# MLP in halved products: sums moved from GpSimd to VectorE, normalisation to ScalarE, third-layer operands written by the second layer

## The reference

```python
h = layernorm(x) * (1 + ca) + sa
x = x + ga * attention(h, W_attn, W_proj)     # 16 heads, causal
h = layernorm(x) * (1 + cb) + sb
a = relu(h @ W1.T + b1)                       # 512 -> 1024
a = relu(a @ W2.T + b2)                       # 1024 -> 1024
x = x + gb * (a @ W3.T + b3)                  # 1024 -> 512
```

## Time and profile before

| | us |
|---|---|
| median of 3 runs | 1684.85 (1684.47 to 1688.04) |
| the profiled execution | 1680.77 |
| its span, first to last instruction | 1679.0 |
| PE busy in it | 1479.9 (88%) |
| DVE busy | 1056.3 (63%) |
| ACT busy | 789.9 (47%) |
| POOL busy | 830.2 (49%) |

### The profile page before, as it was taken

One profiled execution on the slowest core, in us unless ns is written; L12 is line 12 of the kernel. 1 busy time (PEld: TensorE's weight loads), 2 busy tenths in 40 slices (PEclk: granted clock), 3 DMA queues, 4 the chain that ended last, 5 costly groups with the idle time before them and its releaser, 6 DMA issues. The chain is left out here.

```text
span 1679.0 us, 30398 instructions
## 1 busy us (share of the span) xinstructions
PE 1479.9 (88%) x12112; PEld 1340.3 (80%) x12112; DVE 1056.3 (63%) x1795; ACT 789.9 (47%) x1430; POOL 830.2 (49%) x661
## 2 busy tenths in 40 slices
PE   7899999999999999746999999679999999676676
PEld 6578888888888888635888888679999999676676
DVE  4477777777777776638566555754444445865665
ACT  2166667676666666713444444443333334321221
POOL 2166756666656566726444455402222225445645
PEclk9899999999999999967999999989999999888788
DMA  6434353534343434152334444423222224343342
GB/s 215 137 84 115 90 129 89 130 89 124 90 116 95 115 90 105 44 207 88 138 138 142 151 160 160 173 85 129 101 106 109 101 101 153 111 169 139 107 166 98
DMA packets 111229, 205.21 MB, mean 122 GB/s; under 512 B 12648, under 2 KB 35176, under 8 KB 111088
## 3 DMA queue, kind: packets, MB, share of 16 engines
q1 hardware_dynamic: 107456, 200.62, 38.7%
q10 hardware_dynamic: 3632, 2.64, 0.5%
HBM read 93.61 MB, written 58.75 MB: 91 GB/s over the span
## 5 line engine op out<-in xcount | busy, mean ns | idle before, releaser
L429 POOL TENSOR_TENSOR prob_lo<-prob,prob_hi 128x512 f16<-128x512 f32 x256 | 296.9, 1165 | 137.9 <-ACT prob L533 137.6
L526 ACT ACTIVATE prob_hi<-key_score 128x512 f16<-128x512 f32 x320 | 191.1, 597 | 127.6 <-PE key_score L824 125.2
L1994 PE MATMUL sum_b<-op,w 128*128 128x256 f32 x1728 | 221.8, 287 | 14.5 <-DVE op L1663 7.3
L1994 PEld LDWEIGHTS sum_b<-op,w 128*128 128x128 f32 x1728 | 215.2, 195 | 15.5 <-DVE op L1663 7.5
L735 PE MATMUL lin<-h_parts,wqkv 128*128 128x512 f32 x768 | 217.7, 407 | 1.1 <-DVE h_parts L578 1.1
L533 ACT ACTIVATE prob<-key_score 128x512 f32<-128x512 f32 x320 | 190.8, 596 | 0.0
L697 DVE TENSOR_REDUCE row_max<-score 128x1 f32<-128x512 f32 (+2 forms) x384 | 180.3, 498 | 12.4 <-PE score L811 11.5
L735 PEld LDWEIGHTS lin<-h_parts,wqkv 128*128 128x128 f32 x768 | 142.3, 194 | 30.1 <-DVE h_parts L578 3.2
L811 PE MATMUL score<-stack 96*128 96x512 f32 (+3 forms) x512 | 155.2, 364 | 0.0
L1994 PE MATMUL sum_e<-op,w 128*128 128x256 f32 x1152 | 148.2, 286 | 5.0 <-DVE w L1751 5.0
L1994 PE MATMUL sum_a<-op,w 128*128 128x256 f32 x1152 | 147.1, 286 | 5.1 <-DVE w L1751 3.1
(11 more groups left out here) (145 smaller groups left out, 3045.3 us busy)
## 6 DMA issues: line engine op xcount, KB each, us to landing
stack<-qk_parts SPq DMA_DIRECT2D x384, 128.0 KB, 2.4
blk<-y_dram SPq DMA_DIRECT2D x64, 512.0 KB, 5.7
y_dram<-u_c SPq DMA_DIRECT2D x32, 512.0 KB, 2.9
x_tiles<-x SPq DMA_DIRECT2D x32, 256.0 KB, 3.6
attn_dram<-o_rows SPq DMA_DIRECT2D x32, 256.0 KB, 2.3
attn_tiles<-attn_dram SPq DMA_DIRECT2D x8, 1024.0 KB, 5.5
res_tiles<-x SPq DMA_DIRECT2D x8, 1024.0 KB, 8.1
x_dram<-res_tiles SPq DMA_DIRECT2D x8, 1024.0 KB, 4.4
```

Of the source, the lines that this page charges most:

```text
L429: nc.gpsimd.tensor_tensor(prob_lo[:, key[1] % 2, u, :], prob[:, u, :], prob_hi[:, key[1] % 2, u, :], ALU.subtract).then_inc(lo_pool, 1)
L526: nc.scalar.activation(prob_hi[:, q % 2, u, :], bank[:], ACT.Exp, scale=SOFTMAX_SCALE, bias=P_SHIFT)
L1994: mm = nc.tensor.matmul(dst, w[:, wl, c, cols], data[:, dl, c, :], start=begin, stop=end, skip_group_check=again)
```

## The change

What it does, piece by piece:

- All operand sums, weight sums, `add_rows`, `add_bias_rows` and `add_gated` go from POOL to DVE. POOL keeps the eight inverse deviations of 128x4.
- `normalise` goes from DVE to ACT: scale is the inverse deviation, bias is minus mean times it (`minus_means`, one small DVE instruction).
- ACT's order at the end of an expand chunk: `modulate` 2 and 3 stand ahead of the relu of block C21, not behind it.
- Layer 2 writes its result as the **seven operands of layer 3** to a new `y2_dram`: blocks C11, C21, C22 as they are (`store_made`) and four sums (`late_sums`, DVE, two pairs in the next chunk). Layer 3 only loads seven operands of 512 KB (`load_late`) and splits them; it has a buffer for each, so operand s of chunk n+1 can be loaded when product s of chunk n is done.
- Gate times b3 is added to x2 in layer 2: x2 of a chunk is loaded, added to on DVE in one instruction of 128x2048, and stored again (`X2_AT`).
- `w2_lo` and `w3_lo` stand at other places, and the sums of w3 come in two steps.

```diff
+RAW_OPS = {0: 0, 3: 2, 6: 3}
+TEMP_OPS = {4: 0, 5: 1}
...
+MADE_OPS = {0: C11, 3: C21, 5: C22}
+SUM_OPS = (2, 4, 1, 6)
+X2_AT = {B + 1: (0, 1), B + 2: (2,), B + 3: (3,), B + 4: (4,), B + 5: (5,), B + 6: (6, 7)}
...
+            def load_x2_rows(k):
+
+                if k:
+                    sp.wait_ge(xs_out, 16 * k)
+                sp.wait_ge(x2_out[k % 2], 16 * (k // 2 + 1))
+                sp.dma_start(x2[:], rows_of(x2_dram, k)).then_inc(xs_in, 16)
                 if k:
                     sp.wait_ge(gb_b3_ready, k)
                 sp.dma_start(gb_row[:], gate_dram[k:k + 1, C:2 * C].to_broadcast([P, C])).then_inc(gb_in, 16)
+
+            def store_x2_rows(k):
+                sp.wait_ge(xs_ready, k + 1)
+                sp.dma_start(rows_of(x2_dram, k), x2[:]).then_inc(xs_out, 16)
...
+            def store_made(n, s):
+
+                sp.wait_ge(relu_done, relu_no(n, MADE_OPS[s], 3) + 1)
+                sp.dma_start(y_view(y2_dram, n - B, s), made[MADE_OPS[s]][:]).then_inc(y2_out[s], 16)
+
...
+            def load_late(n, s):
+
+                k = n - CONTRACT * B
+                if k:
+                    sp.wait_ge(prod_done, done_no(n - 1, s, 0) + 1)
+                elif s in (0, 5):
+                    sp.wait_ge(op_sum, sum_no(n - 1, 3) + 1)
+                    sp.wait_ge(op_ready, op_no(n - 1, {0: 0, 5: 6}[s]) + 1)
+                elif s == 6:
+                    sp.wait_ge(op_ready, op_no(n - 1, 5) + 1)
+                else:
+                    sp.wait_ge(prod_done, done_no(n - 1, 5 if s == 2 else 4, 1) + 1)
+                sp.wait_ge(y2_out[s], 16 * (k + 1))
+                sp.dma_start(late_whole[s][:, 1], y2_dram[k, s].rearrange("p (c n) -> p c n", n=HB))\
+                    .then_inc(late_in[s], 16)
 
...
             def contract(n):
                 k = n - CONTRACT * B
+                if k == 0:
+                    for i in SUM_OPS:
+                        store_sum(n - 1, i)
+                if k + 1 < B:
+                    load_late(n + 1, 0)
+                    load_late(n + 1, 1)
                 if k:
                     store_out(k - 1, 0)
-                else:
-                    store_block(n - 1, C12)
                 if k and k + 1 < B:
                     load_gate(k + 1)
                 if k + 1 < B:
-                    load_block(n + 1, 0)
-                    load_block(n + 1, 1)
+                    load_late(n + 1, 2)
+                    load_late(n + 1, 3)
                 if k and k + 1 < B:
                     load_x2(k + 1)
                 if k + 1 < B:
-                    load_block(n + 1, 2)
-                    load_block(n + 1, 3)
+                    load_late(n + 1, 4)
+                    load_late(n + 1, 5)
+                    load_late(n + 1, 6)
                 store_out(k, 1)
 
             for k in range(B):
...
+            def normalise(k):
+                act.wait_ge(minus_mean, k + 1)
+                act.wait_ge(x2_ready, NT * (k + 1))
+                if k:
+                    act.wait_ge(aux_done, AUX_NO[(ROWS, k - 1, 3)] + 1)
+                for t in range(NT):
+                    nc.scalar.activation(xn[:, t, :], xt[:, k % 2, t, :], ACT.Identity, scale=rstd[:, t:t + 1],
+                                         bias=shift[:, t:t + 1]).then_inc(x_norm, 1)
 
...
-                    w2_hi(0)
+                if k + 1 < B:
+                    normalise(k + 1)
                 relu(n, C11)
                 hi(n, 6)
                 for c in (0, 1):
                     if k + 1 < B:
                         modulate(k + 1, c)
+                relu(n, C22)
                 if last:
-                    w2_hi(1)
-                relu(n, C22)
+                    w2_hi(0)
                 hi(n + 1, 0)
-                relu(n, C21)
                 for c in (2, 3):
                     if k + 1 < B:
                         modulate(k + 1, c)
+                relu(n, C21)
+                if last:
+                    w2_hi(1)
                 hi(n + 1, 1)
 
...
+            def add_rows(k, t):
+
+                if t == 0:
+                    dve.wait_ge(x_in[k % 2], 16 * (k // 2 + 1))
+                dve.wait_ge(proj_taken, NT * k + t + 1)
+                nc.vector.tensor_tensor(xt[:, k % 2, t], xt[:, k % 2, t], gated[:, t % 2], ALU.add)\
+                    .then_inc(x2_ready, 1)
...
+            def minus_means(k):
+
                 dve.wait_ge(rstd_ready, k + 1)
                 if k:
-                    dve.wait_ge(aux_done, AUX_NO[(ROWS, k - 1, 3)] + 1)
-                for t in range(NT):
-                    nc.vector.tensor_scalar(xn[:, t, :], xt[:, k % 2, t, :], mean_var[:, t, 0:1], rstd[:, t:t + 1],
-                                            ALU.subtract, ALU.mult).then_inc(x_norm, 1)
+                    dve.wait_ge(x_norm, NT * k)
+                nc.vector.scalar_tensor_tensor(out=shift[:], in0=mean_var[:, :, 0], scalar=-1.0, in1=rstd[:],
+                                               op0=ALU.mult, op1=ALU.mult).then_inc(minus_mean, 1)
...
+            def first_op_sum(n):
+
+                block_wait(dve, n, 1)
+                block_wait(dve, n, 0)
+                if n:
+                    dve.wait_ge(op_ready, op_no(n - 1, 4) + 1)
+                nc.vector.tensor_tensor(temp_view(n, 0), block(n, 1), block(n, 0), ALU.subtract).then_inc(op_sum, 1)
...
+            def second_op_sums(n):
+                block_wait(dve, n, 3)
+                ring_wait(dve, n, 1)
+                dve.wait_ge(op_sum, sum_no(n, 0) + 1)
+                nc.vector.tensor_tensor(op_whole(n, 1), block(n, 3), temp_view(n, 0), ALU.subtract).then_inc(op_sum, 1)
+
+                block_wait(dve, n, 2)
+                if n:
+                    dve.wait_ge(op_ready, op_no(n - 1, 5) + 1)
+                dve.wait_ge(op_sum, sum_no(n, 1) + 1)
+                nc.vector.tensor_tensor(temp_view(n, 1), op_whole(n, 1), block(n, 2), ALU.subtract).then_inc(op_sum, 1)
+
+            def third_op_sum(n):
+                ring_wait(dve, n, 2)
+                nc.vector.tensor_tensor(op_whole(n, 2), block(n, 3), block(n, 1), ALU.subtract).then_inc(op_sum, 1)
+
+            def late_sums(n, which):
+
+                k = n - B
+                if which == 0:
+                    dve.wait_ge(relu_done, relu_no(n, C12, 3) + 1)
+                    if k:
+                        dve.wait_ge(y2_out[2], 16 * k)
+                    nc.vector.tensor_tensor(s3[:], c11[:], u2[:], ALU.subtract).then_inc(y_sum, 1)
+                    dve.wait_ge(y_sum, 4 * k + 1)
+                    nc.vector.tensor_tensor(u2[:], u2[:], p1[:], ALU.add).then_inc(y_sum, 1)
+                else:
+                    dve.wait_ge(y_sum, 4 * k + 2)
+                    if k:
+                        dve.wait_ge(y2_out[1], 16 * k)
+                    nc.vector.tensor_tensor(s2[:], u2[:], c11[:], ALU.subtract).then_inc(y_sum, 1)
+                    dve.wait_ge(y_sum, 4 * k + 3)
+                    if k:
+                        dve.wait_ge(y2_out[6], 16 * k)
+                    nc.vector.tensor_tensor(s4[:], u3[:], s2[:], ALU.subtract).then_inc(y_sum, 1)
+
+            def add_bias_rows(k):
+
+                dve.wait_ge(gb_in, 16 * (k + 2))
+                if k:
+                    dve.wait_ge(xs_ready, k)
+                nc.vector.tensor_tensor(gb_b3[:], gb_row[:], b3_rows[:], ALU.mult).then_inc(gb_b3_ready, 1)
+                dve.wait_ge(xs_in, 16 * (k + 1))
+                dve.wait_ge(gb_b3_ready, k + 1)
+                nc.vector.tensor_tensor(x2[:], x2[:], gb_b3[:].unsqueeze(1).broadcast_to([P, NT, C]), ALU.add)\
+                    .then_inc(xs_ready, 1)
 
...
+            def add_gated(n, i):
+                k = n - CONTRACT * B
+                if i == C11:
+                    dve.wait_ge(x2_in[k % 2], 16 * (k // 2 + 1))
+                rows, cols = BLOCKS[i]
+                dst = x2t[:, k % 2, 2 * rows:2 * rows + 2, HB * cols:HB * cols + HB]
+                dve.wait_ge(g_done, 4 * k + RELU_ORDER.index(i) + 1)
+                nc.vector.tensor_tensor(dst, dst, part(made[i], n, 0).rearrange("p (m n) -> p m n", n=HB), ALU.add)\
+                    .then_inc(add_done, 1)
+
             for half in range(2):
                 proj_lo(half)
...
                     w2_lo(6)
                 lo(n, 6)
+                for k in extra[1:]:
+                    add_bias_rows(k)
                 if n == B:
                     w2_lo(5)
-                if n == CONTRACT * B - 1:
-                    for s in range(3):
+                if last:
+                    w3_sum(1)
+                    for s in range(2):
                         w3_lo(s)
                 make_c22(n)
                 lo(n + 1, 0)
-                if n == CONTRACT * B - 1:
-                    for s in range(3, STEPS):
+                if last:
+                    for s in range(2, 4):
                         w3_lo(s)
                 make_c21(n)
+                if last:
```

(12 more changed lines are left out.)

446 lines of the change are left out of this document (220 added, 226 removed).

## The result

The changed kernel takes 1569.74 us (median of 4 runs, 1568.6 to 1571.65), the kernel before 1684.66 us measured beside it. The ratio is 0.9316, with a 95% interval from 0.9299 to 0.9332. The forecast was 1571 us with a range from 1553 to 1602; the measured time is 1.3 us less than forecast. The profiled execution took 1568.6 us, its span is 1566.8 us, 112.2 us less than the span of before.

A forecast was written before the change was run, and what follows sets the result against it. TensorE was taken to bound the second layer, and nearly the first; a loop through SP and POOL the third. Terms summing to 114.2 us off the 1679.0 us span gave a median of 1571 us, range 1553 to 1602.

The forecast's parts named there:

- Third layer: Third layer: sums and loop go, TensorE is the largest load, chunks take 21.1 us in place of 31; 69.6 us gained.
- loop through SP and POOL: Third layer before: block loads, POOL's sums and adds, output store, then SP's next loads; one turn takes 31 us.
- First layer: First layer: modulate 2 and 3 ahead of C21's relu end the projection's wait; chunks 35.3 us, 26.5 us gained.
- Start: Start of the first layer: the four normalisations move to ACT and finish at 760.1 in place of 763.2; 3.2 us gained.
- First to second layer: Change from first to second layer: shorter product waits and two falls of the clock saved; 10 us, bounds 0 and 14.
- Second layer: Second layer: DVE takes on sums and x2 passes without delaying TensorE; 0, up to 4 us lost in chunks 9 and 14.
- all waits stay covered: Second layer: by the layout of DVE's work, TensorE waits for none of it; 0 us, about 28 of 40 us busy.
- Second to third layer: Change from second to third layer: one wait 8.2 in place of 7.8, two others gone; 2.6 us, bounds -6 and 8.
- (a): Third layer: DMA bounds it, at 250 GB/s a chunk takes 24.1 us; +21, 1592 us; chance 0.14.
- (b): First layer: the wait only moves and the clock falls again, the 26.5 us shrink to 5; 1592 us; chance 0.13.
- (c): Changes of layer: they get longer as DVE makes all low parts and sums in one row; +12 to +25, 1590; chance 0.08.
- (d): Third layer, load_late: loads don't overlap, 48.3 us a chunk; +190, 1761 us, slower than before; chance 0.02.

The follow-up runs named there:

- lo_first: Changed kernel with low part 1 ahead of C12's gate and add in the third layer, and the second layer's second x2 pass behind make_c22; 1558.38 us.
- more_loads_4: Changed kernel with four more loads of 512 KB in each third-layer chunk, into a tile that nothing reads; 1567.91 us.
- before_store_later: Kernel before, with the third layer's block loads issued on SyncE ahead of the previous chunk's output store and the x2 load; 1655.45 us.
- order_back: Changed kernel with ScalarE's activation of block C21 put back ahead of the last two slices of modulated rows in the first layer; 1588.49 us.
- norm_on_dve: Changed kernel with the normalisation back on VectorE, one instruction for each of the four rows tiles; 1564.74 us.
- before_two_orders: Kernel before, with modulated rows ahead of block C21 on ScalarE and block loads ahead of the store in the third layer; 1627.58 us.
- pool_beside: Changed kernel with seven sums of 128x1024 added on GpSimd in each third-layer chunk, which no engine waits for; 1611.17 us.
- before_order_only: Kernel before, with only the last two slices of modulated rows moved ahead of block C21 on ScalarE; 1655.04 us.
- combined: Changed kernel with lo_first's moves, low parts 1 to 3 ahead of the late sums at the third layer's start, and normalisation on VectorE; 1549.04 us.
- more_loads_7: Changed kernel with seven more loads of 512 KB in each third-layer chunk; 1616.6 us.

## Why the prediction was right, step by step

**Third layer, 69.6 us forecast, 70.9 measured.** The chunk is 20.90 us (forecast 20.8, taken as 21.1 for transfers that collide). Product 1 waits 0.49 us (0.5 to 0.6), the cause being the one named: make_c12, gate, add and low part 1 in a row, as `lo_first` shows. The allowance for colliding transfers was not needed, as `more_loads_4` shows. What I called a loop through SP and POOL is confirmed in part: the store in it was worth 25 us here (`before_store_later`), and the loop that was left ran through blocks that came free late and GpSimd's sums. Which part of the change removed that one is not shown.

**First layer, 26.5 us for the wait of the projection and 1.7 for the wait behind it (28.2), 31.5 measured.** The chunk is 35.04 us (forecast 35.3), product 6 waits 0.26 us (0.5), ROWS doesn't wait. The sum itself missed some: 0.88 us of wait at the last chunk's product 0 also went, and the wait in the first chunk gave all of its 3.05 us. The price of the lower clock was right for the kernel before (five chunks of 39.6 us became 35.04, 4.6 us each, of which 3.05 are wait), but a wait at that place doesn't always bring it: `order_back` pays it in two of its six chunks.

**Start, 3.2 us forecast, 5.4 measured.** The wait for the normalised rows fell from 14.44 to 11.29 us, the 3.2 us forecast. The other 2.3 us lie in what follows: shorter waits, and a projection that ran at full clock (5.76 us for 24 matmuls, 7.08 before). That clock was luck in part, since three of nine executions of changed kernels didn't have it and were 1 to 2 us longer here. Right in sum, but the part on ScalarE was not what helped (`norm_on_dve`).

**First to second layer, 10 us forecast, 11.0 measured.** Product 1 of the last first-layer chunk waits 4.15 us (4.2 forecast), product 0 of chunk 8 2.33 (2.5), its product 1 5.65 (4.5), product 2 0.72 (0.8).

**Second layer, 0 forecast, 5.7 us lost.** This is the term that missed. The text allowed up to 4 us for chunks 9 and 14, and chunk 14 took 3.7: make_c22 stood behind the second x2 pass of the chunk, whose gate row came late (6.65 us of idle time on VectorE), so that product 6 waited 2.04 us and its 48 matmuls ran 7.46 us instead of 5.92. I had laid out VectorE's load, 28 of 40 us, and not the landing of that one transfer. 1.5 us more are the lower clock at 1085.67, behind a wait of 1.98 us that before had as well, at full clock. The rest, 0.4 us, is chunk 9, with a wait of 0.21 us. The step that failed is thus "all waits stay covered": the layout had a price for the passes and none for the landing of what they wait for, nor for a change of clock behind a wait that stays.

**Second to third layer, 2.6 us forecast, 2.8 measured.** Product 1 of chunk 16 waits 7.54 us (8.2), products 6 of chunk 15 and 1 of chunk 17 don't wait for the old reasons.

The MLP part became 116.6 us shorter where 114.2 were forecast. The 4.4 us by which attention happened to be longer in the profiled execution offset that. That the sum comes so close is luck in part: the other terms gave 8.1 us more than forecast, and the second layer and attention took 10.1 us back. None of the rivals came true: no product waits for a load (a), no wait for norm_tiles inside the first layer (b), both changes of layer got shorter (c), the loads overlap (d).

The one thing that the prediction did not see is how the gain divides. Two edits of order, on ScalarE and on SyncE, give half of it, 3.4% of the 6.8%, with the sums where they were (`before_two_orders`).

## What to carry to other kernels

Before work is moved to another engine, look at what stands ahead of the awaited instruction in its queue: one activation on ScalarE and one store on SyncE held 60 us here, and from the orders alone 28 and 20 us were forecast for them, where 33 and 30 came. Elementwise work on GpSimd is paid twice, once by it and once by the VectorE instructions with two inputs in SBUF beside it, so price it by `pool_beside`'s rows and not by GpSimd's own busy time. When a wait is made shorter where two engines are full, as at the first change of layer, sum their work over the stretch first: the wait goes to the next product.

## What the runs showed that I had not expected

- A wait of about 2 us sometimes lowers TensorE's clock and sometimes doesn't. Product 5 of chunk 8 waits 1.98 us in both kernels; its 48 matmuls then take 6.01 us before and 7.52 after. Of the thirteen profiled executions five have the full clock there (`before`, `before_order_only`, `before_store_later`, `norm_on_dve`, `combined`) and eight the lower one. In `order_back` 2.56 us of wait leave the full clock in four chunks (5.69 us for 24 matmuls of 512 columns) and lower it in two (7.33); the 3.05 us of the kernel before lower it all six times (7.07 to 8.58). No run here tells what decides it.
- One tensor_scalar of 128x512 takes 0.48 us on VectorE alone and 2.5 us beside GpSimd's sums, five times as much, though it has one tensor as input. Low parts with two inputs only double, to about the same length (2.24 us in `pool_beside`); an instruction of GpSimd is as long, 2.34 to 2.61 us. No run here tells why the form with one tensor is held too.
- Transfers of mostly 512 KB gave 388 GB/s over 105 us (`more_loads_4`), and single slices of 3 us up to 423 GB/s (`more_loads_7`). The Trainium skill has about 435 GB/s as the aggregate of a core's DMA engines ("Perfetto Trace Analysis", section "Roofline"); the highest slices come within 3% of it.
- The end of attention, with unchanged code, moved by 7.4 us between executions, more than several of the differences that the experiments were about.
